# Expert stage of a four-layer conv/attention network: the next chunk's queries and scores move between the scattered half tiles, and ten pairs instead of twelve stand ahead of the turning

## The chip, the cores and the metric

One Trainium2 chip, one NeuronCore in use. The metric is device time of one execution in microseconds (us). Engines are written as in the profile: PE is TensorE's matmuls, PEld its weight loads, DVE is VectorE, ACT is ScalarE, POOL is GpSimd, SP the queue that starts DMAs. Instructions of one engine run in order; between engines only semaphores order the work.

## The reference, cut to what matters

The network is a residual convolution, a channel attention, and two layers each of attention and feed-forward on 3136 tokens of 256 channels. The change lies in the feed-forward of the first of these two layers, a product-key mixture of 4096 experts:

```python
q = (x_norm @ wq).reshape(B, T, HEADS, 2, DIM_KEY)          # 8 heads, 2 halves, 32
sim = jnp.einsum('bthpd,hkpd->pbthk', q, keys)              # 64 keys per half
s1, i1 = jax.lax.top_k(sim[0], K)                           # K = 16
s2, i2 = jax.lax.top_k(sim[1], K)
final_scores, pk = jax.lax.top_k(all_scores, K)             # of the 16 x 16 sums
hidden = jax.nn.gelu(jnp.einsum('btd,bthkd->bthk', x_norm, wd), approximate=False)
hidden = hidden * jax.nn.relu(final_scores)
out = jnp.einsum('bthk,bthkd->btd', hidden, wu)
```

## The kernel before

The function is peer_ffn. It doesn't gather experts. For each chunk of 256 tokens it computes the activation of all 4096 experts, multiplies it by a dense matrix of weights that is zero except at the chosen experts, and multiplies the product by the second expert matrix. There are 12 whole chunks (numbered 0 to 11) and a last one of 64 tokens (number 12). A chunk is two tiles of 128 tokens and four half tiles of 64 tokens; experts lie as 128 partitions by J = 32 columns, and two columns make a "pair", so there are NPAIR = 16 pairs.

What each engine does for chunk n, in its own order:

- PE: `hidden` for the first EARLY = 12 pairs (L1576, 8 matmuls a pair, into four PSUM buffers x_ps); `queries` of chunk n+1 (L1554, into sim_ps); `turn` for each tile (L1585), which transposes the codes of the chosen experts and their weights; `hidden` for the remaining 4 pairs; then four times `scatter` (L1600 and L1601, 128 small matmuls that build the weight matrix of a half tile from one-hot operands in the same four x_ps buffers, a quarter of the half tile in each), with `scores` of chunk n+1 (L1563) behind each of the first two; last `experts_out` (L1611, 128 matmuls).
- ACT: the Gelu of each pair (L1680) into g; `query_out` (L1659), which copies the queries of chunk n+1 from sim_ps to qt; the copies of the turned codes (L1694: wh_t, a_t, b_t); the later Gelus; `score_out` for each tile (L1666), which copies scores to sc; and, for the last two half tiles, the copy of each scattered quarter from PSUM (L1702) to one of two buffers m_copy. These two buffers are the two halves of qt, so they can be written only after both `scores` of chunk n+1 have read qt. m_copy k can be written only after POOL is through with copy k-2.
- DVE: `low_weights` (L1839) for tile 0; `one_hots` for four half tiles (L1861, L1863, L1866, L1868), which write the operands of `scatter`, and between the parts of the second and third also `weigh` (L1875), the product of g and the scattered weights of the half tile before; then `top_halves` of chunk n+1 (L1720, L1725, L1727: top 16 of each half's scores) for each tile; `make_codes` of chunk n+1, which ends in L1833 and L1834; and the addition of the output (L1902).
- POOL: for the last two half tiles, the product of g and m_copy (L1540, eight of them in a chunk); the sums of candidates (L1513) and index steps for chunk n+1.
- SP: the load of xc for chunk n+2, once all 16 pairs of chunk n are done.

`experts_out` waits for all products of DVE and POOL. `turn` of chunk n+1 waits for its codes from `make_codes`. The first half tile of a chunk's `scatter` waits for the Gelu of all 16 pairs, since it uses the same PSUM buffers. Chunks come two to a body, and chunks 2 to 9 run in a loop.

Of the kernel before, what the change touches and what calls it, by code (L numbers as in the profile page):

```python
# [22 lines left out]
def wait(eng, semaphore, value):  # L23

    if isinstance(value, int) and value <= 0:
        return
    eng.wait_ge(semaphore, value)
# [1325 lines left out]
def peer_ffn(nc, x, xn_dram, w, ident):  # L1353
# [28 lines left out]
    with Scope(nc, "peer") as S:  # L1382
# [52 lines left out]
        pad = S.sb("pad", [1, 1 + 3 * NTILE])  # L1435
        block = S.block()
        NPAIR = J // 2
        EARLY = 12
        JS = 8
        stage = [g[:, 0:10, :].rearrange("p j t -> p (j t)")[:, 0:JS * C], g[:, 10:20, :].rearrange("p j t -> p (j t)")[:, 0:JS * C]]  # L1440

# [15 lines left out]
        def tile_rows(tokens):  # L1457

            return [min(TT, tokens - t0) for t0 in range(0, tokens, TT)]
# [87 lines left out]
        def _(pe):  # L1547
            def queries(n, p, cols):

                pe.wait_ge(xc_in[p], 8 * (n - p) + 16)  # L1550
                wait(pe, sim_ready, NTILE * n)
                for m in range(4):
                    for k in range(KC):
                        mm = nc.tensor.matmul(sim_ps[m // 2][:, (m % 2) * CT:(m % 2) * CT + cols], wq[:, k, m * P:(m + 1) * P],  # L1554
                                              xc[p][:, k, 0:cols], start=(k == 0), stop=(k == KC - 1))
                mm.then_inc(q_done, 1)

            def scores(n, t, rows):
                pe.wait_ge(q_ready, n + 1)
                if t > 0:  # L1560
                    pe.wait_ge(sim_ready, NTILE * n + t)
                for m in range(4):
                    mm = nc.tensor.matmul(sim_ps[m // 2][0:rows, (m % 2) * 4 * NK:(m % 2 + 1) * 4 * NK], qt[:, m, t * TT:t * TT + rows],  # L1563
                                          keys_b[:, m, :], start=True, stop=True)
                mm.then_inc(sim_done, 1)

            def hidden(n, p, pairs, cols):
                for jp in pairs:
                    b = jp % 4
                    if jp < 4:  # L1570
                        wait(pe, m_copied, 4 * (NHB - LATE) * n - 3 + jp)
                    else:
                        pe.wait_ge(gelu_done, NPAIR * n + jp - 3)
                    for jj in range(2):
                        for k in range(KC):
                            mm = nc.tensor.matmul(x_ps[b][:, jj * CT:jj * CT + cols], dt[:, k, 2 * jp + jj, :], xc[p][:, k, 0:cols],  # L1576
                                                  start=(k == 0), stop=(k == KC - 1))
                    mm.then_inc(h_done, 1)
# [58 lines left out]

            def chunk(n, p, now, then):
                hidden(n, p, range(EARLY), now)
                if then > 0:  # L1640
                    queries(n + 1, 1 - p, then)
                for t, rows in enumerate(tile_rows(now)):
                    turn(n, t, rows)
                hidden(n, p, range(EARLY, NPAIR), now)
                next_rows = tile_rows(then)
                for hb in range(now // HT):
                    scatter(n, hb)
                    if hb < len(next_rows):
                        scores(n + 1, hb, next_rows[hb])
                experts_out(n, now)  # L1650
            chunks(pe, chunk)

        @block.scalar
        def _(act):
            act.preload_act_table(ACT.Gelu)
            def query_out(n, cols):
                act.wait_ge(q_done, n + 1)
                for b in range(2):
                    ins = nc.scalar.activation(qt[:, 2 * b:2 * b + 2, 0:cols],  # L1659
                                               sim_ps[b][:, 0:2 * CT].rearrange("p (m t) -> p m t", m=2)[:, :, 0:cols], ACT.Copy)  # L1660
                ins.then_inc(q_ready, 1)

            def score_out(n, t, rows):
                act.wait_ge(sim_done, NTILE * n + t + 1)
                for b in range(2):
                    ins = nc.scalar.activation(sc[t][0:rows, 8 * b:8 * b + 8, :], sim_ps[b][0:rows, :].rearrange("p (g k) -> p g k", g=8), ACT.Copy)  # L1666
                ins.then_inc(sim_ready, 1)

            query_out(0, CT)
            for t in range(NTILE):  # L1670
                score_out(0, t, TT)
            for i in range(16):
                act.wait_ge(w_turned, i + 2)
                nc.scalar.activation(dt[:, :, 2 * i:2 * i + 2, :].rearrange("p k j e -> p j k e"),
                                     x_ps[i % 4][:, :].rearrange("p (j k e) -> p j k e", j=2, k=KC), ACT.Copy).then_inc(w_out, 1)

            def hidden_out(n, pairs, cols):
                for jp in pairs:
                    act.wait_ge(h_done, NPAIR * n + jp + 1)
                    nc.scalar.activation(g[:, 2 * jp:2 * jp + 2, 0:cols], x_ps[jp % 4][:, 0:2 * CT].rearrange("p (j t) -> p j t", j=2)[:, :, 0:cols],  # L1680
                                         ACT.Gelu).then_inc(gelu_done, 1)

            def chunk(n, p, now, then):
                wait(act, out_done, n)
                hidden_out(n, range(EARLY), now)
                if then > 0:
                    query_out(n + 1, then)
                for t, rows in enumerate(tile_rows(now)):
                    act.wait_ge(tr_done, NTILE * n + t + 1)
                    ts = slice(t * TT, t * TT + rows)  # L1690
                    if t == 0:
                        wait(act, oh_ready, NHB * n)
                    for dst, c in ((wh_t, 2), (a_t, 0), (b_t, 1)):
                        ins = nc.scalar.activation(dst[:, ts, :], tr_ps[:, c * TT:c * TT + rows].unsqueeze(2).broadcast_to([P, rows, R]), ACT.Copy)  # L1694
                    ins.then_inc(tr_ready, 1)
                hidden_out(n, range(EARLY, NPAIR), now)
                for t, rows in enumerate(tile_rows(then)):
                    score_out(n + 1, t, rows)
                for k in range(4 * max(0, now // HT - LATE)):
                    act.wait_ge(m_done, 4 * NHB * n + 4 * LATE + k + 1)  # L1700
                    wait(act, g_done_late, 4 * (NHB - LATE) * n + k - 1)
                    nc.scalar.activation(m_copy[k % 2], x_ps[k % 4][:, 0:GT * J], ACT.Copy).then_inc(m_copied, 1)  # L1702
            chunks(act, chunk)

        @block.vector
# [583 lines left out]
```

## Time and profile before

| what | us |
|---|---|
| median of 3 runs | 2588.43 |
| lowest and highest run | 2580.5, 2592.27 |
| the profiled execution, its own time | 2570.97 |
| span of its trace | 2569.3 |
| mean granted TensorE clock over the span | 0.866 |
| the expert stage's chunks within the span, about | 640 to 1975 |

Times in the rows are counted from the start of the span. A chunk's round is read best from one `turn` of tile 0 to the next. An idle time in brackets is that of the engine just before the row, with what ended it.

### The profile page before, as it was taken

What the parts mean: (1) busy time and instruction counts of PE and PEld (TensorE: products, weight loads), DVE (VectorE), ACT (ScalarE), POOL (GpSimd) and SP (SyncE); (2) the same over time, 40 slices, a digit from 0 to 9 for tenths busy, and PEclk for the clock granted to TensorE, in tenths of its full rate; (3) what the DMA queues carried; (4) which work ended last, traced back from release to release, by engine and by line L of the source; (5) the groups of instructions that cost most, each with busy time, mean ns of one, the idle gap of its engine ahead of it and who ended that gap; (6) DMA issues with size and microseconds to landing.
All of it is one profiled execution on the core that took longest, in us unless ns stands there. A gap on an engine that the chain in (4) does not pass through costs nothing. (4 is left out here: it accounts for less than half of the span.)

```text
span 2569.3 us, 48752 instructions
## 1 busy us (share of the span) xinstructions
PE 1949.0 (76%) x17712; PEld 1582.6 (62%) x17712; DVE 1741.8 (68%) x7029; ACT 674.3 (26%) x1478; POOL 520.4 (20%) x670
## 2 busy tenths in 40 slices
PE   6585999963785966868678687786977898539993
PEld 3464788842675766757567576675767676226663
DVE  4334666646798898998989989899982786440003
ACT  2442455442212202122021221212211355302120
POOL 2003444311023031220302203023031210040004
PEclk8786999986888989979798897988976799759996
DMA  2103444217000000000000000000000332232233
GB/s 56 32 23 91 107 106 106 68 39 162 5 1 6 5 2 5 2 6 5 2 6 1 6 6 2 5 1 3 1 1 11 88 85 56 88 103 91 91 96 106
DMA packets 86758, 107.70 MB, mean 42 GB/s; under 512 B 26462, under 2 KB 75230, under 8 KB 85790
## 3 DMA queue, kind: packets, MB, share of 16 engines
q1 hardware_dynamic: 81056, 96.62, 14.2%
q0 software_dynamic: 3296, 6.43, 1.0%
q8 instruction: 141, 2.31, 0.4%
q10 hardware_dynamic: 2176, 1.61, 0.2%
q14 instruction: 89, 0.73, 0.1%
HBM read 70.61 MB, written 30.51 MB: 39 GB/s over the span
## 5 line engine op out<-in xcount | busy, mean ns | idle before, releaser
L1611 PE MATMUL peer_out_ps<-peer_g,peer_up 128*128 128x256 f32 (+1 forms) x1664 | 391.1, 404 | 62.8 <-issue 56.8
L1611 PEld LDWEIGHTS peer_out_ps<-peer_g,peer_up 128*128 128x128 f32 x1664 | 338.9, 214 | 111.3 <-issue 62.9
L1576 PE MATMUL peer_x_ps<-peer_xc,peer_dt 128*128 128x256 f32 (+1 forms) x1664 | 358.8, 377 | 27.3 <-DMA peer_up<-in_L_ffn_expert_up_dram 19.1
L1540 POOL TENSOR_TENSOR peer_g<-peer_g,peer_qt 128x512 f32<-128x512 f32 x96 | 213.2, 2256 | 791.8 <-ACT peer_qt L1702 791.8
L1576 PEld LDWEIGHTS peer_x_ps<-peer_xc,peer_dt 128*128 128x128 f32 x1664 | 310.7, 194 | 70.3 <-issue 29.0
L1600 PE MATMUL peer_x_ps<-peer_oh_h,peer_oh_a 128*128 128x32 bf16 x3136 | 171.5, 184 | 206.8 <-DVE peer_oh_l L1868 194.6
L1600 PEld LDWEIGHTS peer_x_ps<-peer_oh_h,peer_oh_a 128*128 128x128 bf16 x3136 | 166.4, 101 | 222.4 <-DVE peer_oh_l L1868 135.9
L1680 ACT ACTIVATE peer_g<-peer_x_ps 128x512 f32<-128x512 f32 (+1 forms) x208 | 119.1, 573 | 649.8 <-PE peer_x_ps L1576 649.7
L1277 DVE TENSOR_REDUCE l_attn_mx<-l_attn_s_ps 98x4 f32<-98x392 f32 (+1 forms) x320 | 175.1, 560 | 141.4 <-PE l_attn_s_ps L1047 100.8
L1861 DVE TENSOR_TENSOR peer_oh_a<-peer_a_t,peer_iota_f 128x8192 bf16<-128x8192 bf16 x49 | 216.7, 4423 | 1.3
L1198 ACT ACTIVATE l_attn_pt<-l_attn_st_ps 98x392 f32<-98x392 f32 x320 | 148.3, 492 | 143.5 <-PE l_attn_st_ps L1060 142.6
L1601 PE MATMUL peer_x_ps<-peer_oh_l,peer_oh_a 128*128 128x32 bf16 x3136 | 170.7, 184 | 0.0
L1601 PEld LDWEIGHTS peer_x_ps<-peer_oh_l,peer_oh_a 128*128 128x128 bf16 x3136 | 166.9, 101 | 0.0
L1725 DVE FIND_INDEX8 peer_i<-peer_v,peer_sc 128x8 uint32<-128x64 f32 (+1 forms) x800 | 166.1, 219 | 0.0
L2224 DVE TENSOR_TENSOR moe_y<-moe_y_ps,moe_b 98x256 f32<-98x256 f32 x32 | 13.6, 425 | 222.7 <-PE moe_y_ps L2098 222.7
L1043 PE MATMUL l_attn_s_ps<-l_attn_stk,l_attn_stq 96*98 96x196 bf16 (+1 forms) x768 | 114.2, 246 | 27.6 <-DMA l_attn_stk<-l_attn_pieces_k_dram 16.9
L972 POOL TENSOR_SCALAR_AFFINE_SELECT l_attn_pt<-l_attn_pt 98x196 f32<-98x196 f32 (+1 forms) x192 | 98.5, 518 | 133.7 <-ACT l_attn_pt L1198 132.3
L1060 PE MATMUL l_attn_st_ps<-l_attn_stq,l_attn_stk 98*98 98x196 bf16 (+1 forms) x768 | 111.4, 243 | 9.5 <-ACT l_attn_pt L1198 4.7
L1720 DVE MAX8 peer_v<-peer_sc 128x8 f32<-128x64 f32 (+1 forms) x800 | 105.9, 208 | 11.3 <-issue 10.0
L2098 PE MATMUL moe_y_ps<-moe_w,moe_h 128*98 128x256 f32 x512 | 111.8, 379 | 0.0
L1702 ACT ACTIVATE peer_qt<-peer_x_ps 128x512 f32<-128x512 f32 x96 | 57.4, 598 | 198.3 <-POOL peer_g L1540 134.4
L2098 PEld LDWEIGHTS moe_y_ps<-moe_w,moe_h 128*98 128x98 f32 x512 | 84.5, 165 | 27.6 <-issue 1.3
(310 smaller groups left out, 3545.5 us busy)
## 6 DMA issues: line engine op xcount, KB each, us to landing
moe_w<-in_L_ffn_w_dram SPq DMA_DIRECT2D x16, 1024.0 KB, 9.1
l_attn_pieces_q_dram<-l_attn_pieces_q SPq DMA_DIRECT2D x16, 294.0 KB, 4.0
l_attn_pieces_k_dram<-l_attn_pieces_k SPq DMA_DIRECT2D x16, 294.0 KB, 2.9
l_attn_stq<-l_attn_pieces_q_dram SPq DMA_DIRECT2D x16, 294.0 KB
l_attn_stk<-l_attn_pieces_k_dram SPq DMA_DIRECT2D x16, 294.0 KB
peer_g<-n_L_ffn_expert_down_dram SPq DMA_DIRECT2D x8, 512.0 KB, 6.5
peer_up<-in_L_ffn_expert_up_dram SPq DMA_DIRECT2D x2, 2048.0 KB
l_xi<-net_x SPq DMA_DIRECT2D x16, 196.0 KB, 2.3
```

The lines of the kernel that those rows point to most:

```text
L1043: mm = nc.tensor.matmul(out[:, j, :], stq[n % NB][0:KS, spot(h), t * TH:(t + 1) * TH], stk[n % NB][0:KS, spot(h), 0:nb * TH], start=(j == ...
L1198: nc.scalar.activation(pt[g % NPT][:, f * FW:(f + 1) * FW], st_ps[i % 2][0:TH, 0:FW], ACT.Exp).then_inc(exp_done, 1)
L1277: nc.vector.tensor_reduce(mx[n % 2][:, hs[0]:hs[0] + len(hs), t], s_ps[i % 2][0:TH, 0:FW].rearrange("p (h j) -> p h j", j=nb * TH), AX_X, ...
L1540: nc.gpsimd.tensor_tensor(g[:, :, ts], g[:, :, ts], m_copy[q % 2].rearrange("p (t j) -> p j t", j=J), ALU.mult).then_inc(g_done_late, 1)
L1576: mm = nc.tensor.matmul(x_ps[b][:, jj * CT:jj * CT + cols], dt[:, k, 2 * jp + jj, :], xc[p][:, k, 0:cols], start=(k == 0), stop=(k == KC - 1))
L1600: nc.tensor.matmul(x_ps[q][:, i * J:(i + 1) * J], oh_a[hb % 2][:, t, :], oh_h[hb % 2][:, t, :], start=True, stop=False)
L1601: mm = nc.tensor.matmul(x_ps[q][:, i * J:(i + 1) * J], oh_a[hb % 2][:, t, :], oh_l[hb % 2][:, t, :], start=False, stop=True)
L1611: mm = nc.tensor.matmul(out_ps[:, m * CT:m * CT + cols], up[:, j, m * P:(m + 1) * P], g[:, j, 0:cols], start=(j == 0), stop=(j == J - 1))
L1680: nc.scalar.activation(g[:, 2 * jp:2 * jp + 2, 0:cols], x_ps[jp % 4][:, 0:2 * CT].rearrange("p (j t) -> p j t", j=2)[:, :, 0:cols], ACT.Ge ...
L1725: last = nc.vector.max_index(indices[:, q, r], values[:, q, r], source)
L1861: nc.vector.tensor_tensor(view(oh_a[q]), spread(a_t, P), number(P), ALU.is_equal)
L2098: mm = nc.tensor.matmul(y_ps[s % 2][0:ST, 0:C], h[p][:, f, s * ST:(s + 1) * ST], w2[p][:, f, :], start=(f == 0), stop=(f == KF - 1))
```

## The change

In PE's order, `queries` of chunk n+1 moves from ahead of the turning to behind the first scattered half tile, and each `scores` moves by one half tile: tile 0's behind the second, tile 1's behind the third. In ACT's order `query_out` moves behind the last Gelus, just ahead of `score_out`. EARLY becomes 10, so that 10 pairs stand ahead of the turning and 6 behind it. No operation is added or taken away.

```diff
-        EARLY = 12
+        EARLY = 10
...
             def chunk(n, p, now, then):
                 hidden(n, p, range(EARLY), now)
-                if then > 0:
-                    queries(n + 1, 1 - p, then)
                 for t, rows in enumerate(tile_rows(now)):
                     turn(n, t, rows)
                 hidden(n, p, range(EARLY, NPAIR), now)
                 next_rows = tile_rows(then)
                 for hb in range(now // HT):
                     scatter(n, hb)
-                    if hb < len(next_rows):
-                        scores(n + 1, hb, next_rows[hb])
+                    if hb == 0 and then > 0:
+                        queries(n + 1, 1 - p, then)
+                    if 0 < hb <= len(next_rows):
+                        scores(n + 1, hb - 1, next_rows[hb - 1])
                 experts_out(n, now)
...
                 hidden_out(n, range(EARLY), now)
-                if then > 0:
-                    query_out(n + 1, then)
...
                 hidden_out(n, range(EARLY, NPAIR), now)
+                if then > 0:
+                    query_out(n + 1, then)
                 for t, rows in enumerate(tile_rows(then)):
                     score_out(n + 1, t, rows)
```

## Rows read from the trace of the kernel before

**Rows 1.** The page, busy time, share of the span and instructions.

```profile
PE 1949.0 (76%) x17712; PEld 1582.6 (62%) x17712; DVE 1741.8 (68%) x7029; ACT 674.3 (26%) x1478; POOL 520.4 (20%) x670
```

**Rows 2.** Busy time by stretch: stretch, length, PE, PEld, DVE, ACT, POOL, clock, DMA.

```profile
640.00:1975.00 1335.00, 1016.72 (x10051) 896.51 (x10051) 1171.76 (x5350) 251.33 (x450) 274.32 (x248) 0.87 0.01 3
```

**Rows 3.** Timeline of PE, one round: start, length, operation, idle before.

```profile
879.87 0.49 PE L1585 MATMUL peer_tr_ps<-net_ident,peer_oh_a 128*128 128x128 f32 x3
...
931.43 30.23 PE L1611 MATMUL peer_out_ps<-peer_g,peer_up 128*128 128x256 f32 x128 [5.18 <-issue]
961.49 20.88 PE L1576 MATMUL peer_x_ps<-peer_xc,peer_dt 128*128 128x256 f32 x96
982.21 3.62 PE L1554 MATMUL peer_sim_ps<-peer_xc,peer_wq 128*128 128x256 f32 x16
985.66 0.49 PE L1585 MATMUL peer_tr_ps<-net_ident,peer_oh_a 128*128 128x128 f32 x3
```

**Rows 4.** Timeline of DVE in the same round.

```profile
882.66 0.69 DVE L1839 TENSOR_TENSOR peer_wl_t<-peer_tr_ps,peer_wh_t 128x512 bf16<-128x512 f32 x1 [7.80 <-ACT peer_b_t L1694]
...
896.26 0.68 DVE L1875 TENSOR_TENSOR peer_g<-peer_g,peer_x_ps 128x512 f32<-128x512 f32 x1
...
912.19 4.43 DVE L1861 TENSOR_TENSOR peer_oh_a<-peer_a_t,peer_iota_f 128x8192 bf16<-128x8192 bf16 x1
916.52 1.23 DVE L1863 TENSOR_TENSOR peer_oh_l<-peer_b_t,peer_iota_f 128x2048 bf16<-128x2048 bf16 x1
917.78 2.40 DVE L1866 TENSOR_TENSOR peer_oh_h<-peer_oh_l,peer_wh_t 128x2048 bf16<-128x2048 bf16 x1
920.10 2.51 DVE L1868 TENSOR_TENSOR peer_oh_l<-peer_oh_l,peer_wl_t 128x2048 bf16<-128x2048 bf16 x1
...
979.74 0.59 DVE L1834 SCALAR_TENSOR_TENSOR peer_oh_a<-peer_oh_a 128x256 f32<-128x256 f32 x1
```

**Rows 5.** Timeline of PE, the scattered half tiles of the same round.

```profile
891.62 0.19 PE L1600 MATMUL peer_x_ps<-peer_oh_h,peer_oh_a 128*128 128x32 bf16 x1 [0.69 <-ACT peer_g L1680]
...
905.08 2.17 PE L1563 MATMUL peer_sim_ps<-peer_keys_b,peer_qt 128*128 128x256 f32 x8
911.81 0.19 PE L1600 MATMUL peer_x_ps<-peer_oh_h,peer_oh_a 128*128 128x32 bf16 x1 [4.56 <-DVE peer_oh_l L1868]
```

**Rows 6.** Timeline of ACT in the same round.

```profile
876.62 0.60 ACT L1680 ACTIVATE peer_g<-peer_x_ps 128x512 f32<-128x512 f32 x1 [1.13 <-PE peer_x_ps L1576]
880.07 1.08 ACT L1659 ACTIVATE peer_qt<-peer_sim_ps 128x512 f32<-128x512 f32 x2 [2.86 <-PE peer_sim_ps L1554]
881.04 0.60 ACT L1694 ACTIVATE peer_wh_t<-peer_tr_ps 128x512 bf16<-128x512 f32 x1
...
907.29 1.09 ACT L1666 ACTIVATE peer_sc<-peer_sim_ps 128x512 f32<-128x512 f32 x2 [9.36 <-PE peer_sim_ps L1563]
912.93 0.60 ACT L1702 ACTIVATE peer_qt<-peer_x_ps 128x512 f32<-128x512 f32 x1 [4.55 <-PE peer_x_ps L1601]
```

**Rows 7.** Timeline of POOL in the same round: the eight products together.

```profile
913.61 17.72 POOL L1540 TENSOR_TENSOR peer_g<-peer_g,peer_qt 128x512 f32<-128x512 f32 x8 [65.07 <-ACT peer_qt L1702]
```

**Rows 8.** The same view in narrow windows: the first, second, and fifth and sixth product.

```profile
913.61 5.49 POOL L1540 TENSOR_TENSOR peer_g<-peer_g,peer_qt 128x512 f32<-128x512 f32 x1 [65.07 <-ACT peer_qt L1702]
...
919.06 2.47 POOL L1540 TENSOR_TENSOR peer_g<-peer_g,peer_qt 128x512 f32<-128x512 f32 x1
...
925.43 2.98 POOL L1540 TENSOR_TENSOR peer_g<-peer_g,peer_qt 128x512 f32<-128x512 f32 x2
```

**Rows 9.** Busy time by stretch in the same round; columns as in the second group.

```profile
931.40:934.00 2.60, 2.57 (x6) 2.14 (x7) 2.56 (x24) 0.00 (x0) 0.00 (x0) 0.50 0.00 0
```

**Rows 10.** Timeline of all engines, the turning of chunk 0.

```profile
668.42 0.49 PE L1585 MATMUL peer_tr_ps<-net_ident,peer_oh_a 128*128 128x128 f32 x3
...
671.21 0.69 DVE L1839 TENSOR_TENSOR peer_wl_t<-peer_tr_ps,peer_wh_t 128x512 bf16<-128x512 f32 x1 [12.74 <-ACT peer_b_t L1694]
```

**Rows 11.** Timeline of PE, the pairs of chunk 12, which has 64 tokens.

```profile
1921.11 10.83 PE L1576 MATMUL peer_x_ps<-peer_xc,peer_dt 128*128 128x64 f32 x96
```

## The prediction

> **What bounds the kernel now.** I read the page first [rows 1]: PE is busy for 76% and DVE for 68% of the span, so no engine is the bound everywhere. The change touches only the expert stage, so next comes busy time by stretch [rows 2]: from 640 to 1975 DVE is busy for 1171.76 of 1335 us and PE for 1016.72. DVE is nearer to full, yet not full. Last come the timelines of one round, from the `turn` of tile 0 at 879.87 to that at 985.66, 105.79 us [rows 3]. I write t for the time since 879.87.
>
> DVE [rows 4] has one large hole in the round: 7.80 us before `low_weights`, at t = 2.79. It had finished its codes and added the output by about 874.9, and then waited for the turned codes. The codes of the next round end at 979.74 + 0.59 = 980.33, while PE turns them at 985.66 [rows 3]. So the turn comes 5.33 us after it could, because PE is not there yet. PE in turn, followed back from 985.66, has no hole: queries 3.45 us (982.21 to 985.66), 12 pairs 20.72 us (961.49 to 982.21), `experts_out` 30.06 us (931.43 to 961.49). In front of that it idles 5.18 us, and the last of POOL's eight products ends at 913.61 + 17.72 = 931.33 [rows 7]. The page of waits calls this idle time "issue", but the product that PE multiplies by became ready 0.1 us before. POOL's eight run without a hole, from the first copy ACT could make of the third half tile (912.93) [rows 6]; that half tile started when DVE's one-hots were ready (911.81, released by L1868) [rows 5].
>
> The round is thus one ring: turn, DVE's one-hots up to the third half tile, POOL's products, `experts_out`, pairs, queries, turn. There is a second ring beside it, DVE alone from turn to codes, which is 5.33 us shorter.
>
> **Two pairs and the queries leave the ring.** Two of 12 pairs are 20.72 / 6 = 3.45 us, the queries 3.45 us. Both are still done, later. The pairs run while DVE makes the first half tile's one-hots. The first half tile started at t = 11.75, released by the Gelu of the last pair [rows 5]; it now starts at about 11.75 + 3.45 = 15.20. DVE first needs its result for `weigh` at 896.26, t = 16.39 [rows 4]; a quarter of 128 matmuls that took about 3.4 us is 0.85 us, so it is ready at about 16.1. Cover is thin there, 0.3 us, but it is enough. Both times move 0.48 earlier by the next term. Queries then follow to about t = 22.3; the second half tile could start at about t = 21.7, so PE is some 0.6 us late, and the third isn't before t = 31.94. PE had idle time of 4.56 us ahead of the third [rows 5], which covers this and the 2 us of scores.
>
> **ACT's copies come earlier.** Before, the two instructions of `query_out` (1.08 us) started 0.20 us after the turn and the copies of the turned codes stood behind them, from 881.04, t = 1.17 [rows 6]. Now a Gelu of 0.60 us stands in their place. It starts as long after the pairs' end as before (876.62 in the round shown), so the copies start 1.08 - 0.60 = 0.48 us sooner. DVE's `low_weights` and all behind it move up by that.
>
> **What the moved scores cost.** m_copy lies in qt. ACT may overwrite it only after `scores` of tile 1, and `score_out` stands ahead of the copies in ACT's order. These scores now stand behind the third half tile: it starts at 911.81, takes about 3.4 us to issue, the scores 2.17 us [rows 5], the two copies of `score_out` 1.09 us, the first m_copy 0.60 us [rows 6]. POOL starts at 911.81 + 3.4 + 2.17 + 1.09 + 0.60 = 919.1 in place of 913.61, 5.5 us late. SP's load for chunk n+2 waits for all 16 pairs and moves by 3 us; it has most of a round.
>
> How much of the 5.5 us reaches `experts_out`? Rows 8 show that the first product took 5.49 us, the second 2.47, the fifth and sixth 1.49 each (2.98 for two). Beside the first lies DVE's L1861 of 4.43 us, and L1866 and L1868 took 2.40 and 2.51 us where L1863, of their size, took 1.23 [rows 4]. The engines hinder each other: POOL gets nothing done before about 917.7, then both crawl. A first product that starts at 919.1 meets only what is left of DVE's one-hots. Upper bound for the delay: the eight take 17.72 us wherever they stand, then it is 5.5 us. Lower bound: DVE, undisturbed until 918.95, ends L1868 at 920.2 and the eight run from there at 1.49 us, to 932.1: delay 0.8 us. If L1868 is slowed to 921.4 and the first product takes 2.47, the end is 919.1 + 2.47 + 7 x 1.49 = 932.0. These two middle readings nearly agree, and I allow for a second slow product (2.47): 933.0, a delay of 1.7. I take 0.9, nearest to the fast rows. Even with scores at half the clock (4.34 us instead of 2.17) POOL starts at 921.3 and would end by 933.2, a delay of 1.9.
>
> The Trainium skill, "SBUF — State Buffer", section "Who interferes with whom", says that VectorE and GpSimd share one pair of ports as an exclusive lock, and that the one that comes second is blocked for the whole instruction. By that rule the 5.49 us are mostly waiting and the delay would be the 0.8 us above; by the plain duration of the row it would be 5.5. The slow pair L1866 and L1868 agrees with a conflict that costs both sides, not with a block of one alone.
>
> **The sum.** The ring shortens by 3.45 + 3.45 + 0.48 - 0.9 = 6.48 us, to 99.3. DVE's own ring was 105.79 - 5.33 = 100.46; the copies give 0.48, and L1866 and L1868 give 1.2 to 2.4 when POOL leaves them alone, so 97.6 to 98.8, under 99.3. PE's ring still decides. If DVE got no relief it would decide, at 100.0, and the gain is 5.8.
>
> Rounds that end in turns 1 to 10 gain 6.48 each, 64.8. Chunk 0 turned at 668.42, DVE having been idle for 12.74 us before 671.21, so its codes were ready at 658.5 [rows 10]; the turn moves by 3.45 + 3.45 = 6.9 to 661.5 and is still behind them. The round that ends in turn 11 has queries of only 64 tokens; in proportion of the pairs' 10.83 to 20.88 us [rows 3, 11] they are 1.8 us, so it gains 4.8. The round to turn 12 loses two pairs of 10.83 / 6 = 1.8 us and has one tile of scores, whose copy is no later: 1.8. After turn 12 nothing changes. Total 64.8 + 6.9 + 4.8 + 1.8 = 78.3 us.
>
> The profiled execution took 2570.97 us for a span of 2569.3; it would take 2492.7. The median of the runs is 17.5 us above it, unexplained by this trace, so I take the gain from the median: 2588.43 - 78.3 = 2510.1. Runs of before spread over 12 us, about 0.5%, which is also what I count as no change.
>
> **The rivals.**
>
> *DVE gets no relief (chance 0.15).* POOL's later products fall on the top 16 searches and slow these as they slowed L1866 and L1868. DVE's ring decides at 100.0 us a round: 10 x 5.8 + 6.9 + 4.8 + 1.8 = 71.5, 2517 us. For it: DVE is the fullest engine. Against: by 925.43 POOL ran at full pace beside DVE's searches.
>
> *POOL's delay arrives whole (0.12).* The eight products still take 17.7 us from 919.1. The round gains 3.45 + 3.45 + 0.48 - 5.5 = 1.9, turn 11's 0.2, together 19 + 6.9 + 0.2 + 1.8 = 28 us: 2560. For it: eight rows summed without a hole. Against: [rows 8], four products at one third of the first one's time.
>
> *Nothing moves (0.06).* If the turn waited for something other than PE's place in line, the ring stays at 105.8, 2588 us; or the moved wait takes all of 6.5. Nothing in DVE's rows speaks for it.
>
> *Slower (0.04): PE's clock.* `experts_out` starts after an idle 5.18 us at a granted clock of 0.50, the 1.2 GHz level [rows 9]; its 128 matmuls take 30.06 us. Now the idle time before it grows by about 3 us, DVE's earlier one-hots included. If that kept the clock down for the whole of `experts_out` and the pairs, these 30.06 + 17.27 us would double at most, +47 us a round, 12 x 40 = 480 slower. It decides against the change from 2 x 6.48 = 13 us more at the low clock. The Trainium skill, "TensorE: Matmul & The Clock Gate", section "HAM oscillation — how this bites in real kernels", says idle gaps bring PE down to half rate and the next work starts cold; by it the change would pay where a gap is lengthened. The rows show that this price is already paid in every round, so only its length can change; I allow 1 us a round either way, 12 us in all.
>
> **How the numbers follow.** The forecast proper has 0.63. Its own range: 10 to 11 rounds by 0.8 us of the delay and 1 us of clock, 2495 to 2528. The range for 8 in 10 takes in the second case and half the way to the third: 2495 to 2545. Faster by over 0.5% are the first three cases, 0.90; within 0.5% 0.06; slower 0.04.
>
> **What would show it.** Turns 99 to 100 us apart; DVE's hole before `low_weights` down from 7.80 to 2.3 to 4 us; L1659 between the first scattered half tile and the second; the first L1540 near t = 39, with a time near 2.5 us or less instead of 5.49, and the eight together in 12 to 14 us; L1866 and L1868 mostly at 1.23; `experts_out` near t = 52. The prediction is wrong if the eight still take 17 us, if DVE's first `weigh` waits for PE, or if `experts_out` takes well over 30 us.

## The result and the profile after

| | before | after |
|---|---|---|
| median, us | 2588.62 (4 runs, 2580.5 to 2592.27) | 2500.2 (4 runs, 2491.81 to 2501.5) |
| ratio to before, 95% interval | | 0.9648 (0.9614 to 0.9682) |
| profiled execution, us | 2570.97 | 2491.81 |
| span, us | 2569.3 | 2490.1 |

The change made the kernel 3.5% faster, 88 us by the medians and 79 us from profiled execution to profiled execution. The forecast was 78 us, to 2510 us, with a range of 2495 to 2545.

One round of PE after, in its timeline, from turn to turn (start, length, operation, idle before), beside [rows 3, 5]:

```profile
863.34 0.49 PE L1585 MATMUL peer_tr_ps<-net_ident,peer_oh_a 128*128 128x128 f32 x3
866.48 0.52 PE L1585 MATMUL peer_tr_ps<-net_ident,peer_oh_a 128*128 128x128 f32 x3 [2.65 <-DVE peer_wl_t L1839]
866.83 10.53 PE L1576 MATMUL peer_x_ps<-peer_xc,peer_dt 128*128 128x256 f32 x48
...
881.26 3.70 PE L1554 MATMUL peer_sim_ps<-peer_xc,peer_wq 128*128 128x256 f32 x16
...
888.00 1.97 PE L1563 MATMUL peer_sim_ps<-peer_keys_b,peer_qt 128*128 128x256 f32 x8
894.79 0.21 PE L1600 MATMUL peer_x_ps<-peer_oh_h,peer_oh_a 128*128 128x32 bf16 x1 [4.81 <-DVE peer_oh_l L1868]
...
898.22 2.52 PE L1563 MATMUL peer_sim_ps<-peer_keys_b,peer_qt 128*128 128x256 f32 x8
903.18 0.21 PE L1600 MATMUL peer_x_ps<-peer_oh_h,peer_oh_a 128*128 128x32 bf16 x1 [2.44 <-DVE peer_oh_l L1868]
...
914.86 30.31 PE L1611 MATMUL peer_out_ps<-peer_g,peer_up 128*128 128x256 f32 x128 [7.21 <-issue]
945.00 17.43 PE L1576 MATMUL peer_x_ps<-peer_xc,peer_dt 128*128 128x256 f32 x80
962.27 0.49 PE L1585 MATMUL peer_tr_ps<-net_ident,peer_oh_a 128*128 128x128 f32 x3
```

The round is 98.93 us instead of 105.79. Queries and both scores stand in what was idle time ahead of the half tiles. `experts_out` starts 51.52 us after the turn, as before (51.56), although POOL starts its products 5.4 us later in the round. ACT, POOL and DVE in the same round show why; they answer to [rows 4, 6 to 8]. ACT's timeline after:

```profile
863.54 0.60 ACT L1680 ACTIVATE peer_g<-peer_x_ps 128x512 f32<-128x512 f32 x1 [1.13 <-PE peer_x_ps L1576]
864.03 0.59 ACT L1692 ACTIVATE peer_wh_t<-peer_tr_ps 128x512 bf16<-128x512 f32 x1
...
900.77 1.08 ACT L1666 ACTIVATE peer_sc<-peer_sim_ps 128x512 f32<-128x512 f32 x2 [9.68 <-PE peer_sim_ps L1563]
901.74 1.09 ACT L1702 ACTIVATE peer_qt<-peer_x_ps 128x512 f32<-128x512 f32 x2
```

POOL's timeline after, the eight products and, in a narrow window, the first:

```profile
902.43 12.33 POOL L1540 TENSOR_TENSOR peer_g<-peer_g,peer_qt 128x512 f32<-128x512 f32 x8 [66.46 <-ACT peer_qt L1702]
...
902.43 2.06 POOL L1540 TENSOR_TENSOR peer_g<-peer_g,peer_qt 128x512 f32<-128x512 f32 x1 [66.46 <-ACT peer_qt L1702]
```

DVE's timeline after:

```profile
861.18 0.60 DVE L1834 SCALAR_TENSOR_TENSOR peer_oh_a<-peer_oh_a 128x256 f32<-128x256 f32 x1
861.62 0.68 DVE L1902 TENSOR_TENSOR net_x<-net_x,peer_out_ps 128x512 f32<-128x512 f32 x1
865.64 0.69 DVE L1839 TENSOR_TENSOR peer_wl_t<-peer_tr_ps,peer_wh_t 128x512 bf16<-128x512 f32 x1 [3.34 <-ACT peer_b_t L1692]
...
900.76 1.22 DVE L1866 TENSOR_TENSOR peer_oh_h<-peer_oh_l,peer_wh_t 128x2048 bf16<-128x2048 bf16 x1
901.90 1.22 DVE L1868 TENSOR_TENSOR peer_oh_l<-peer_oh_l,peer_wl_t 128x2048 bf16<-128x2048 bf16 x1
```

POOL's eight products take 12.33 us instead of 17.72, L1866 and L1868 take 1.22 us instead of 2.40 and 2.51, and the copies of the turned codes start 0.69 us after the turn instead of 1.17. The codes were ready at 861.78, 1.56 us ahead of the turn (5.33 before); DVE's hole is 3.34 us instead of 7.80.

The other place that changed is the last chunk, which has 64 tokens. Its `experts_out` in PE's timeline, before and after, with busy time by stretch over the same us (length, PE, PEld, DVE, ACT, POOL, clock, DMA):

```profile
1946.19 27.57 PE L1611 MATMUL peer_out_ps<-peer_g,peer_up 128*128 128x64 f32 x128 [0.78 <-DVE peer_g L1875]
1946.20:1973.80 27.60, 27.56 (x128) 27.37 (x128) 0.01 (x1) 0.00 (x0) 0.00 (x0) 0.50 0.00 1
...
1869.12 14.51 PE L1611 MATMUL peer_out_ps<-peer_g,peer_up 128*128 128x64 f32 x128 [0.78 <-DVE peer_g L1875]
1869.10:1883.60 14.50, 14.48 (x128) 14.37 (x128) 0.00 (x0) 0.00 (x0) 0.00 (x0) 1.00 0.00 1
```

The same 128 matmuls take 14.51 us at full granted clock instead of 27.57 us at half of it. In both kernels they start 14.32 us after the turn of chunk 12.

### The profile page after: what moved, and what is told of

Its sections match the earlier page's. It is cut to its first block and busy times, and to the rows that moved or that the text cites. A ratio compares the mean times of both kernels' runs of the same rounds, so it can differ in the third digit from the quotient of the medians.

```text
span 2490.1 us, 48756 instructions
## 1 busy us (share of the span) xinstructions
PE 1924.0 (77%) x17712; PEld 1559.4 (63%) x17712; DVE 1714.5 (69%) x7029; ACT 670.6 (27%) x1478; POOL 461.2 (19%) x670
## 3 DMA queue, kind: packets, MB, share of 16 engines
q8 instruction: 141, 2.31, 0.4%
## 5 line engine op out<-in xcount | busy, mean ns | idle before, releaser
L1611 PE MATMUL peer_out_ps<-peer_g,peer_up 128*128 128x256 f32 (+1 forms) x1664 | 377.9, 392 | 84.7 <-issue 76.8
L1611 PEld LDWEIGHTS peer_out_ps<-peer_g,peer_up 128*128 128x128 f32 x1664 | 325.8, 203 | 133.2 <-issue 84.8
L1576 PE MATMUL peer_x_ps<-peer_xc,peer_dt 128*128 128x256 f32 (+1 forms) x1664 | 355.0, 374 | 26.7 <-DMA peer_up<-in_L_ffn_expert_up_dram 19.1
L1576 PEld LDWEIGHTS peer_x_ps<-peer_xc,peer_dt 128*128 128x128 f32 x1664 | 308.1, 192 | 68.5 <-issue 28.5
L1540 POOL TENSOR_TENSOR peer_g<-peer_g,peer_qt 128x512 f32<-128x512 f32 x96 | 154.1, 1643 | 802.4 <-ACT peer_qt L1702 802.4
L1861 DVE TENSOR_TENSOR peer_oh_a<-peer_a_t,peer_iota_f 128x8192 bf16<-128x8192 bf16 x49 | 216.6, 4420 | 1.3
L1043 PE MATMUL l_attn_s_ps<-l_attn_stk,l_attn_stq 96*98 96x196 bf16 (+1 forms) x768 | 112.9, 244 | 30.6 <-DMA l_attn_stk<-l_attn_pieces_k_dram 18.3
L2098 PEld LDWEIGHTS moe_y_ps<-moe_w,moe_h 128*98 128x98 f32 x512 | 84.5, 165 | 27.6 <-issue 1.3
L1081 PE MATMUL l_attn_o_ps<-l_attn_pt,l_attn_va 98*32 98x196 f32 (+1 forms) x1536 | 92.9, 312 | 9.3 <-DVE l_attn_o L1284 8.8
```

The costliest lines, as they stand in the source:

```text
L1043: mm = nc.tensor.matmul(out[:, j, :], stq[n % NB][0:KS, spot(h), t * TH:(t + 1) * TH], stk[n % NB][0:KS, spot(h), 0:nb * TH], start=(j == ...
L1540: nc.gpsimd.tensor_tensor(g[:, :, ts], g[:, :, ts], m_copy[q % 2].rearrange("p (t j) -> p j t", j=J), ALU.mult).then_inc(g_done_late, 1)
L1611: mm = nc.tensor.matmul(out_ps[:, m * CT:m * CT + cols], up[:, j, m * P:(m + 1) * P], g[:, j, 0:cols], start=(j == 0), stop=(j == J - 1))
L1861: nc.vector.tensor_tensor(view(oh_a[q]), spread(a_t, P), number(P), ALU.is_equal)
L2098: mm = nc.tensor.matmul(y_ps[s % 2][0:ST, 0:C], h[p][:, f, s * ST:(s + 1) * ST], w2[p][:, f, :], start=(f == 0), stop=(f == KF - 1))
```

## The experiments

Each was timed beside the kernel before. "Turns" is the time from the first turn of chunk 0 to that of chunk 12 in the profiled execution; "stage" is the time from that first turn to the stage's last instruction, so it holds chunk 12 as well, but not the pairs ahead of that first turn, some 1.7 us each; "rounds" is the range of the eight shortest of the eleven rounds between whole chunks (the other three are 0.1 to 7 us longer, mostly where a pass of the loop begins). Kernels with one letter shared a chip.

| kernel | chip | ratio to before (95%) | turns, us | stage, us | rounds, us |
|---|---|---|---|---|---|
| before | | 1 | 1263.5 | 1305.7 | 104.1 to 106.2 |
| changed | | 0.9648 (0.9614 to 0.9682) | 1189.0 | 1218.2 | 98.7 to 100.1 |
| e1: only the pairs | A | 0.9835 (0.9813 to 0.9857) | 1236.8 | 1265.9 | 100.7 to 104.4 |
| e2: only queries and scores | A | 0.9851 (0.9827 to 0.9875) | 1228.8 | 1271.0 | 102.4 to 102.8 |
| e3: only scores of tile 1 | A | 1.0005 (0.9989 to 1.0022) | 1263.7 | 1306.0 | 104.2 to 106.1 |
| e4: both scores behind the second half tile | A | 0.9741 (0.9709 to 0.9774) | 1209.6 | 1238.7 | 99.6 to 101.4 |
| e5: nine pairs ahead | B | 0.9746 (0.9723 to 0.9768) | 1218.1 | 1247.3 | 101.9 to 102.4 |
| e6: eight pairs ahead | B | 0.9780 (0.9756 to 0.9803) | 1217.1 | 1259.3 | 100.8 to 102.5 |
| e7: changed, output split by tile | B | 0.9594 (0.9571 to 0.9617) | 1172.5 | 1212.3 | 97.3 to 99.4 |
| e9: before, output split by tile | B | 0.9763 (0.9741 to 0.9784) | 1204.6 | 1246.7 | 99.9 to 100.5 |
| e8: e7 with twelve pairs ahead | C | 0.9635 (0.9614 to 0.9657) | 1171.1 | 1213.4 | 97.2 to 97.8 |
| e10: e7 with thirteen pairs ahead | C | 0.9607 (0.9577 to 0.9637) | 1177.1 | 1206.2 | 97.2 to 98.9 |
| e11: changed again | C | 0.9632 (0.9613 to 0.9651) | 1189.4 | 1218.5 | 98.9 to 100.3 |
| e12: e7 again | D | 0.9609 (0.9586 to 0.9632) | 1172.0 | 1211.8 | 97.2 to 99.2 |

**e1 and e2, the two halves of the change.** e1 is before with `EARLY = 10`, e2 the changed kernel with `EARLY = 12`:

```diff
-        EARLY = 12
+        EARLY = 10
```

> The kernel before with ten pairs ahead of the turning, queries and scores left where they were. Ring theory: a round shortens by two pairs alone, 3.45 us, from 105.8 to about 102.3; POOL's eight products still start beside DVE's one-hots and take 17.7 us. Over all rounds 10 x 3.45 + 3.45 at the start + 3.45 + 1.8 = 43 us, ratio to before about 0.983. Rival, all of the gain comes from POOL's shorter products: no change here, ratio 1.00.

> The changed kernel with twelve pairs ahead of the turning again: only queries, query_out and scores are moved. Ring theory: 3.45 us for the queries and 0.04 net (0.48 from ACT's earlier copies less 0.44 from POOL's later end) a round, 105.8 to about 102.3; 40 us in all, ratio about 0.985, and with the run that changes only the pairs it adds up to the whole gain. POOL's eight products take about 12.3 us. Rival, all from POOL's shorter products: the whole gain of the changed kernel here, ratio 0.965.

The ratios came out as the ring theory has it, 0.9835 against 0.983 and 0.9851 against 0.985, and the rival, all of the gain from POOL, falls with both: in e1 POOL and DVE stay as slow together as before, and the kernel is 1.65% faster all the same. But e1's ratio is right in part by luck. Its turns gained 26.7 us where the expectation's terms behind the first turn give 39.8; another 13.1 us came from chunk 12, whose `experts_out` ran at full clock in e1, as in the changed kernel, and not in e2. e2's turns gained 34.7 us of the 36.7 that its expectation comes to behind the first turn. These are e1's rows of the view by groups (busy us, mean ns | idle before):

```profile
L1540 POOL TENSOR_TENSOR peer_g<-peer_g,peer_qt 128x512 f32<-128x512 f32 x96 | 213.0, 2254 | 762.8 <-ACT peer_qt L1702 762.8
L1868 DVE TENSOR_TENSOR peer_oh_l<-peer_oh_l,peer_wl_t 128x2048 bf16<-128x2048 bf16 x49 | 75.1, 1532 | 0.0
L1839 DVE TENSOR_TENSOR peer_wl_t<-peer_tr_ps,peer_wh_t 128x512 bf16<-128x512 f32 (+1 forms) x25 | 16.9, 677 | 75.1 <-ACT peer_b_t L1694 75.1
```

The two halves add up to 3.1% of 3.5 to 3.7%; in the turns they add up to 26.7 + 34.7 = 61.4 of 74.5 us. e1's rounds vary more than the others' (100.7 to 110.5 us). Where its six pairs behind the turn took 10.53 us and no pass of the loop begins, a round is 102.4 to 102.6 us, near the 102.3 expected (100.7 to turn 11, which has short queries); in six of its twelve rounds they took 11.6 to 13.0 us, and DVE waited 1.1 to 2.5 us for the first half tile. A table behind the experiments has this for all kernels.

**e3, POOL's later start alone.**

```diff
-                    if hb < len(next_rows):
-                        scores(n + 1, hb, next_rows[hb])
+                    if hb in (0, 2) and hb // 2 < len(next_rows):
+                        scores(n + 1, hb // 2, next_rows[hb // 2])
```

> The kernel before, with only the scores of tile 1 moved behind the third half tile; queries ahead of the turning, twelve pairs. POOL then starts 5.5 us later and nothing else leaves the ring. If the two engines only hindered each other before (my reading), the eight products take about 12.3 us instead of 17.7, L1866 and L1868 take 1.23 us each, the round lengthens by 0.4 to 0.9 us, and the kernel by 5 to 10 us, ratio 1.002 to 1.004. If POOL's delay arrives whole: 5.5 us a round, 60 us, ratio 1.023.

The time doesn't move, 1.0005, and neither do the turns. I had expected 1.002 to 1.004: POOL does end 0.48 us later, but `experts_out` takes 0.2 to 0.65 us less in each round between whole chunks. The rival, 1.023, is outside the interval by far. The groups show the exchange, where before had 213.2 us for the first line and 75.3 and 74.0 for L1868 and L1866:

```profile
L1540 POOL TENSOR_TENSOR peer_g<-peer_g,peer_qt 128x512 f32<-128x512 f32 x96 | 158.1, 1688 | 879.4 <-ACT peer_qt L1702 879.4
L1866 DVE TENSOR_TENSOR peer_oh_h<-peer_oh_l,peer_wh_t 128x2048 bf16<-128x2048 bf16 x49 | 61.0, 1245 | 0.9
L1868 DVE TENSOR_TENSOR peer_oh_l<-peer_oh_l,peer_wl_t 128x2048 bf16<-128x2048 bf16 x49 | 61.0, 1244 | 0.0
```

Starting POOL 5.4 us later in each of 11 chunks, about 60 us in all, removes 55 us of its products' time and 27 us of DVE's. DVE's relief is worth nothing here, since PE decides.

**e4, the opposite: POOL starts early again.** In the changed kernel both scores stand behind the second half tile:

```diff
-                    if 0 < hb <= len(next_rows):
-                        scores(n + 1, hb - 1, next_rows[hb - 1])
+                    if hb == 1:
+                        for t, rows in enumerate(next_rows):
+                            scores(n + 1, t, rows)
```

> The changed kernel with the scores of both tiles behind the second half tile, so that ACT can copy the third half tile at once and POOL starts some 5.5 us earlier, beside DVE's one-hots again. By my reading of the contention POOL's eight take 17.7 us again and end about 0.4 us earlier, but L1866 and L1868 take 2.4 and 2.5 us, so DVE's own ring grows from 97.4 to about 99.8 us and passes PE's 98.5: the round becomes 99.8 instead of 98.9, the kernel some 10 us slower than the changed one, ratio to before about 0.969. Rival, an earlier start of POOL is worth its 5.5 us or a good part of it: rounds of 97.4 to 98.4 us, ratio 0.960 to 0.963.

Direction and mechanism hold: L1867 and L1869, which are L1866 and L1868 here, take 73.9 and 75.1 us again. PE waits for codes now, a wait that the changed kernel's list doesn't have. The size was too small: ratio 0.9741, not 0.969. The end of one round in the timeline of all engines of e4:

```profile
969.87 0.59 DVE L1835 SCALAR_TENSOR_TENSOR peer_oh_a<-peer_oh_a 128x256 f32<-128x256 f32 x1
...
970.52 0.55 PE L1585 MATMUL peer_tr_ps<-net_ident,peer_oh_a 128*128 128x128 f32 x3 [0.95 <-DVE peer_oh_a L1835]
```

And e4's DVE behind the turn before it:

```profile
886.40 0.69 DVE L1876 TENSOR_TENSOR peer_g<-peer_g,peer_x_ps 128x512 f32<-128x512 f32 x1 [1.41 <-PE peer_x_ps L1601]
```

Here DVE's first `weigh` waits 1.41 us for PE, which it did not in the changed kernel's round. In this round of e4 the six pairs behind the turn took 12.21 us instead of 10.53. In the four rounds where they took 10.53 and no pass of the loop begins, the round was 99.7 to 100.0 us, the 99.8 that I expected; what I missed is the seven rounds in which they took longer.

**e5 and e6, nine and eight pairs ahead** in the changed kernel.

> The changed kernel with nine pairs ahead of the turning. PE's ring loses another pair, 1.73 us, down to 97.2; but seven pairs then stand ahead of the first half tile, which starts at about t = 16.4 after the turn, so that DVE's first product of it (due at t = 15.9) waits about 1.4 us for the first quarter. Both rings pass through that wait: PE's 98.6, DVE's 97.4 + 1.4 = 98.8. The round stays at 98.6 to 98.9, time within 0.2% of the changed kernel (ratio to before 0.963 to 0.966). Rival, only PE's ring counts and DVE has room: 1.5 us a round more, ratio 0.958.

> The changed kernel with eight pairs ahead of the turning. The first half tile starts another 1.73 us later, DVE's first product waits about 3.1 us: PE's ring 98.9 - 3.45 + 3.1 = 98.6, DVE's 97.4 + 3.1 = 100.5, which decides. Rounds of 100.5, 17 us slower than the changed kernel, ratio to before about 0.972. Rival, DVE has room: no slower than with ten pairs, ratio 0.958 to 0.965.

The expected turning point is there, but my size for e5 was wrong: its rounds are 102, not 98.8 us. PE's timeline of e5, the turn and the seven pairs behind it:

```profile
866.76 0.52 PE L1585 MATMUL peer_tr_ps<-net_ident,peer_oh_a 128*128 128x128 f32 x3 [2.31 <-DVE peer_oh_a L1834]
...
870.51 14.00 PE L1576 MATMUL peer_x_ps<-peer_xc,peer_dt 128*128 128x256 f32 x56
```

The other engines' timeline of e5, DVE's first product and, later, POOL's first:

```profile
886.20 0.69 DVE L1875 TENSOR_TENSOR peer_g<-peer_g,peer_x_ps 128x512 f32<-128x512 f32 x1 [3.51 <-PE peer_x_ps L1601]
...
908.82 1.50 POOL L1540 TENSOR_TENSOR peer_g<-peer_g,peer_qt 128x512 f32<-128x512 f32 x1 [68.10 <-ACT peer_qt L1702]
908.87 2.53 DVE L1868 TENSOR_TENSOR peer_oh_l<-peer_oh_l,peer_wl_t 128x2048 bf16<-128x2048 bf16 x1
```

Busy time by stretch of e5 (length, PE, PEld, DVE, ACT, POOL, clock, DMA):

```profile
870.00:882.50 12.50, 12.50 (x51) 10.73 (x51) 12.47 (x6) 4.56 (x8) 0.00 (x0) 0.84 0.01 1
```

PE idles 2.31 us for the codes and 2.56 us for the second turn. After that its granted clock is 0.84 on average over the 12.5 us shown, so part of it was at the 1.2 GHz level. The wait for codes isn't needed for this: in the four rounds of e5 that began without one, with only the wait for the second turn, the seven pairs took 13.8 to 13.9 us. The seven pairs take 14.00 us where six took 10.53 at full clock in the changed kernel (12.3 for seven). DVE's first product then waits 3.51 us, not 1.4. And because the half tiles are spaced otherwise, POOL's first product happens to start 0.05 us ahead of L1868, which costs DVE 1.3 us more. 1.7 us (clock) + 0.4 (in the wait beside it) + 1.3 make 3.4 of the 3.6 us that I missed; the second term is only what is left over of the wait. In e6 DVE's waits for the first product sum to 53.3 us against 42.7 in e5, but L1868 takes 61.0 us again instead of 75.4, and the two come to nearly the same sum of rounds. e6's forecast of 100.5 us a round held where the clock stayed up: in four rounds the eight pairs took 13.98 us and the round 100.7 to 100.8. In the other eight they took 15.2 to 15.7 us, and rounds without a loop pass in them were 102.2 to 102.5; so e6's turns are 28.1 us longer than the changed kernel's, not 17, and chunk 12's `experts_out` at half clock adds another 13: ratio 0.978, not 0.972.

**e7 and e9, output split by tile.** PE's wait for POOL becomes room for the output of the first 128 tokens, which needs only DVE's products:

```diff
-                pe.wait_ge(g_done_late, 4 * (NHB - LATE) * n + 4 * max(0, n_hb - LATE))
                 wait(pe, x_done, n)
-                for m in range(KC):
-                    for j in range(J):
-                        mm = nc.tensor.matmul(out_ps[:, m * CT:m * CT + cols], up[:, j, m * P:(m + 1) * P], g[:, j, 0:cols],
-                                              start=(j == 0), stop=(j == J - 1))
+                for t, rows in enumerate(tile_rows(cols)):
+                    if t == 1:
+                        pe.wait_ge(g_done_late, 4 * (NHB - LATE) * n + 4 * max(0, n_hb - LATE))
+                    for m in range(KC):
+                        o = m * CT + t * TT
+                        for j in range(J):
+                            mm = nc.tensor.matmul(out_ps[:, o:o + rows], up[:, j, m * P:(m + 1) * P], g[:, j, t * TT:t * TT + rows],
+                                                  start=(j == 0), stop=(j == J - 1))
```

> The changed kernel with the output matmuls split by tile of tokens: the 128 matmuls of 256 columns become 256 of 128 columns, and those of tile 0 don't wait for POOL's products. PE then works in the 7.2 us that it idles for POOL. PE's ring falls by some 6 to 8 us, DVE's ring of 97.4 us decides: rounds of 97.4 to 97.7 us, 13 to 17 us faster than the changed kernel, ratio to before about 0.959. DVE's idle time before low_weights falls from 3.3 to about 2 us. Rival, the narrower matmuls cost more than the idle time gives (weight loads of 128 rows bound them): PE's ring doesn't fall under 98.9, ratio 0.965 or more.

> The kernel before with the output matmuls split by tile of tokens and nothing else changed. If PE's wait for POOL and DVE's ring are what I think, PE's ring of 105.8 loses the 5.2 us in which it idled for POOL and most of the cold start, less some for the narrower matmuls, and DVE's ring at 100.3 us (with POOL's contention in it) decides or nearly decides: rounds of 100 to 101 us, 50 to 60 us faster than before, ratio 0.977 to 0.98. It would reach about two thirds of the change's gain by another way. Rival, as above: 103 or more, ratio over 0.99.

e7 has 0.9594 against 0.959 expected, e9 0.9763 against 0.977 to 0.98, with rounds of 100 to 100.5 us. e9 takes another piece out of the same ring of PE and stops at the same other ring, DVE's. e7's turns are 16.5 us shorter than the changed kernel's. PE's timeline of e7:

```profile
858.40 0.88 PE L1585 MATMUL peer_tr_ps<-net_ident,peer_oh_a 128*128 128x128 f32 x3 [6.48 <-DVE peer_oh_a L1837]
...
862.51 11.63 PE L1576 MATMUL peer_x_ps<-peer_xc,peer_dt 128*128 128x256 f32 x48
```

Busy time by stretch around e7's turn, columns as above:

```profile
857.90:862.50 4.60, 1.54 (x6) 1.20 (x7) 2.08 (x4) 1.57 (x3) 0.00 (x0) 0.50 0.00 0
```

PE now idles 6.48 us for codes, turns at a granted clock of 0.50 (0.88 us instead of 0.49), and its six pairs take 11.63 us instead of 10.53; DVE's first product waits 1.14 us in this round. DVE is the bound, and PE's slower pairs make DVE's ring longer: this happened in all nine rounds of e7 that begin with a wait for codes, and in none of the other three.

**e8, e10, e11 and e12, more pairs ahead and the repeats.**

> The changed kernel with the output matmuls split by tile of tokens and twelve pairs ahead of the turning. With ten pairs this kernel's PE idled 6.5 us for the codes, turned and ran the following pairs partly at a granted clock of 0.5 (six pairs took 11.6 us instead of 10.5), and DVE waited 1.1 us in its first product; rounds were 97.3 to 99.4 us. Theory now: twelve pairs fill half of that idle time, only four stand ahead of the first half tile, DVE's wait in its first product goes to zero and its own ring stands bare: rounds of 97.3 to 97.6 us each, 10 to 15 us faster than with ten pairs, ratio to before about 0.954. Rival, the pairs' place doesn't matter once DVE decides: same as with ten pairs, 0.959.

> As the one before, with thirteen pairs ahead of the turning. PE's idle time for the codes falls by another 1.7 us, to about 1 to 2 us, so the clock stays at its upper level across the turning; DVE's ring decides all the same: rounds of 97.3 to 97.5 us, within 0.2% of twelve pairs. Rival, PE's ring is longer than I think: each pair more costs 1.7 us a round, 0.7% slower than twelve.

> The changed kernel once more, beside the two others on the same chip: rounds of 98.9 us, ratio to before 0.965, as when it was first timed.

> The changed kernel with the output matmuls split by tile of tokens and ten pairs ahead of the turning, once more, since it was timed against another series of the kernel before than the changed kernel's second timing (0.9632). If it is faster than the changed kernel, its ratio is again 0.957 to 0.962 and its rounds 97.3 to 99.4 us; if the first timing flattered it, 0.963 or more.

Within the stage e8 did what I expected of a round (97.2 to 97.8 us in eight rounds) but not of the whole. DVE's first product never waits, as expected. Three rounds, where passes of the loop begin, were 99.5, 102.7 and 103.7 us, with the pairs ahead of the turn taking 25.2 to 26.9 us instead of 20.9. The turns add up to 1171.1 us, level with e7's 1172.5, and the kernel is no faster than the changed one (0.9635 against 0.9632 on the same chip). The profiled executions show where its gain of 18.3 us in the turns over e11 went: 13.1 us into `experts_out` of chunk 12, at half clock in e8 and at full clock in e11, and 8.3 us into a later first turn, of which its two more pairs are 3.5 and the rest lies ahead of the stage. e10 has the ratio 0.9607; its turns are longer than those of e7 and e8 (1177.1), but its chunk 12 ran at full clock, and its stage is the shortest of all, 1206.2 us, with three more pairs ahead of it than e7 has (5.2 us). e12 came at 0.9609, and its interval overlaps that of the changed kernel's repeat, 0.9613 to 0.9651. So splitting the output is likely worth some 6 us beyond the change, as in the stage of e7 and e12: 17 us in the turns (1172 in both executions against 1189 in both of the changed kernel's) less 11 in chunk 12. Which of e7 and e10 is the faster isn't shown; their intervals overlap.

**The pairs behind the turning, in all rounds.** From the timelines of the 14 profiled executions, twelve rounds each: the time that the pairs behind the turn took, and how long DVE's first `weigh` then waited for PE.

| pairs behind | rounds at full clock | pairs, us | wait, us | rounds partly at 1.2 GHz | pairs, us | wait, us |
|---|---|---|---|---|---|---|
| 3 | 3 | 5.34 | 0 | 9 | 6.6 to 7.2 | 0 |
| 4 | 30 | 7.07 | 0 | 30 | 8.1 to 9.7 | 0 |
| 6 | 37 | 10.53 | 0 | 35 | 11.5 to 13.0 | 1.05 to 2.5 |
| 7 | 0 | | | 12 | 13.8 to 14.1 | 3.1 to 3.7 |
| 8 | 4 | 13.98 | 3.2 | 8 | 15.2 to 15.7 | 4.7 to 5.0 |

So six pairs behind the turn, as in the changed kernel, fit only at full clock; four fit at either level. The changed kernel paid in two of its twelve rounds, e1 in six, e7 in nine. What sets the clock down is told only in part. All 49 rounds that began with a wait for codes of more than 1.25 us ran partly at the low level, and 8 of the 16 with a shorter wait, but so did 37 of the 103 that began with none, where PE idled only for the second turn. The changed kernel has both: the same idle time of 2.64 or 2.65 us, then 10.53 us for the six pairs at 863.34 and 11.70 us here, in the round whose turn is at 1063.84 (PE's timeline, busy time by stretch, DVE's timeline):

```profile
1067.64 11.70 PE L1576 MATMUL peer_x_ps<-peer_xc,peer_dt 128*128 128x256 f32 x48
1066.60:1079.30 12.70, 12.33 (x51) 10.48 (x51) 12.56 (x7) 4.56 (x8) 0.00 (x0) 0.87 0.01 1
1081.03 0.69 DVE L1875 TENSOR_TENSOR peer_g<-peer_g,peer_x_ps 128x512 f32<-128x512 f32 x1 [1.21 <-PE peer_x_ps L1601]
```

## Why the prediction was right, and where not

**The ring** was read rightly. Turn to turn, forecast 99.3, measured 98.93. Two pairs and the queries: 3.45 + 3.45, and e1 and e2 show each by itself in the rounds in which PE kept its full clock. ACT's copies: forecast 0.48 us earlier, measured 1.17 - 0.69 = 0.48.

**The cover of the first half tile** was forecast as thin, 0.3 us, but enough. It was enough in ten of twelve rounds. In the other two, of 100.02 and 99.88 us, DVE's first `weigh` waited 1.21 and 1.10 us for PE, which the prediction had named as a sign of being wrong. The forecast took the two moved pairs at their time at full clock and had no term for the clock there.

**POOL's delay** was forecast at 0.9 us between 0.8 and 5.5. POOL ended 51.42 us after the turn and before 51.46; with the 0.48 us that all moved ahead, the delay is 0.44 us. That POOL's lost time comes from DVE, and not from the products themselves, was argued from [rows 4, 8] and is shown by e3. My text said that a conflict costs both sides and is not a block of one alone. That was half wrong: in the changed kernel the first product takes 2.06 us beside an undisturbed L1868 of 1.22 that started 0.53 us ahead of it, and in e5 the product takes 1.50 and L1868 2.53 when POOL was 0.05 us ahead. Each time one runs at full pace and the other waits. [rows 4, 8] already fit this if the engines take turns: POOL's first product waits for L1861 and L1863 to 917.75 and ends at 919.10, and L1866, started at 917.78, ends at 920.18, its undisturbed 1.2 us behind that. The Trainium skill, "SBUF — State Buffer", section "Who interferes with whom", says that the ports that the two engines share are an exclusive lock, and that the order of issue decides who blocks. The trace agrees, with these 2.06 and 2.53 us.

**DVE's ring** was forecast at 97.6 to 98.8 and measured at 98.93 - 1.56 = 97.37. The relief came whole. The rival in which DVE decides didn't occur, but it stands 1.6 us behind, and e4 to e6 show it deciding in most of their rounds.

**The clock** of `experts_out` moved nothing: 30.14 us from its start to the first pair, 30.06 before, though the idle time ahead grew from 5.18 to 7.21 us. The slower rival fell. But the clock moved time in two other places, for which the prediction has no term: at the pairs behind the turning, by the table above, and at `experts_out` of chunk 12, where the change gained 13.1 us by it. The Trainium skill, "TensorE: Matmul & The Clock Gate", section "HAM oscillation — how this bites in real kernels", says that idle gaps bring PE down to half rate. The trace agrees behind each of the 49 longer waits for codes; the 103 rounds without one went both ways.

**The sum.** Rounds to turn 12: forecast 64.8 + 4.8 + 1.8 = 71.4, measured 1263.5 - 1189.0 = 74.5. The first ten rounds gained 68.5, not 64.8, and the last gained 0.8, not 1.8. Chunk 0's stretch before its turn shrank from 26.09 (642.33 to 668.42) to 19.01 us (646.78 to 665.79), 7.1 against 6.9; but it began 4.45 us later, behind the load of the second expert matrix, so the turn came only 2.6 us sooner. After turn 12 the prediction has "nothing changes". By the trace the whole part was 637.4 before and 635.3 after, but it is the sum of three differences: chunk 12 was 13.1 us shorter (42.2 to 29.1, its `experts_out` at full clock), the attention behind it 4 us shorter (262.1 to 258.1), and the mixture feed-forward at the end, counted from PE's first instruction in it, 15.0 us longer (333.1 to 348.1). Together that is the 79.2 us between the spans, and that it is so near to the forecast 78.3 is luck: a gain of 13 us that the forecast put at nothing and a loss of 15 us in code that no kernel here touches nearly cancel. Where the change acts, the gain is 7.1 us ahead of the first turn and 1305.7 - 1218.2 = 87.5 us from there to the end of the stage, 94.6 us against the 78.3 forecast.

**What stays open.** Why chunk 12's `experts_out` gets the full clock in one kernel and half of it in another isn't shown. It starts 14.3 us after the turn in all 14 executions. It took 27.6 us in before, e2, e3, e6, e8 and e9, 14.5 in changed, e1, e4, e5, e10 and e11, and 25.2 in e7 and e12, so the two kernels that were profiled twice repeat; but by pairs ahead, eight and twelve are at half clock, nine and thirteen at full clock, and ten is either. Nor does the idle time of PE ahead of chunk 12's half tile order them: 5.83 us in before and 2.26 in e6 (half clock), 4.05 in changed and 6.73 in e10 (full clock). So these 13 us can't be counted as earned by the moved work.

The mixture stage took 331.8 to 333.1 us in before and in the four kernels of chip B, and 346.1 to 349.2 in all others. The median of before is 2575.2 on chip B and 2587.3 to 2590.1 on the other three. So this stage is likely most of the 17.65 us by which before's profiled execution lies under its median of 2588.62. It is the same code each time; 11 of the 15 us lie in its last stretch, PE's transposes of L2109, which took 30.1 us in before and 41.3 in changed. What makes the difference wasn't tested. With equal mixture stages the two profiled executions would lie 79.2 + 15.0 = 94.2 us apart, against 88.4 by the first medians and 95.3 by e11's.

## What to carry to other kernels

Find the ring that closes a loop round, take out of it what nobody in it needs, and put that into the holes that the same engine already has; then compute the second ring, since that is where the next step stops. A consumer that starts later can end at the same time if its early start only fought another engine for the memory. Work that moves behind a point that the second ring also passes needs cover there at either clock: with four pairs behind the turning DVE never waited, with six it waited in 35 of 72 rounds, and nine pairs ahead instead of ten cost 1%. And a ratio that agrees with a forecast isn't yet the mechanism: e1's did, with nearly a third of its gain from a place that the forecast didn't have.

## What the runs showed of the hardware

- POOL's product of two SBUF operands (1.49 us) and DVE's bf16 `tensor_tensor` (1.22 us) exclude each other. Started 0.53 us behind, POOL took 2.06 us; started 0.05 us behind, DVE took 2.53.
- Behind a wait for codes of over 1.25 us (up to 7.3) and the 2.6 us wait for the second turn, PE's granted clock was at or partly at the 1.2 GHz level in 49 of 49 rounds (six pairs took 11.63 us instead of 10.53 in e7's round). With no wait for codes and only the wait for the second turn, 66 of 103 rounds stayed at full clock (six pairs in 10.53 us) and 37 did not (11.70 us in the changed kernel's round from 1063.84).
- The same 128 matmuls of 64 columns took 14.51 us at a granted clock of 1.00 and 27.57 us at 0.50, a factor of 1.9.
- Between executions of kernels with equal code there, the mixture feed-forward took 331.8 to 333.1 us in five and 346.1 to 349.2 in nine; the four that shared chip B are all among the five.
